# Last attention layer of a two-layer model: slots of eight heads with two blocks each, all scores of a slot together

## The reference

```
def _L1_ffn_ref(x, Wa, Wp, w_std, w_rec):           # C = 512, 16 heads of D = 32 (24 + 8)
    col_scale = concat([repeat(s_std, 24), repeat(s_std, 24), ones(C), repeat(s_rec, 8), repeat(s_rec, 8)])
    fused = x @ (Wa * col_scale)                    # Q_std, K_std, V, Q_low, K_low
    q_tail = where(w_rec > 0.1, K_low, Q_low)       # k_tail the other way round
    Qf, Kf = concat([Q_std, q_tail]), concat([K_std, k_tail])
    scores = Qf @ Kf.T * scale, masked causally (112 x 112 for each head)
    y = softmax(scores) @ V, heads side by side
    return y @ Wp
x = x + tanh(g_ffn[1]) * _L1_ffn_ref(_layernorm(x), Wa, Wp, w_std, w_rec)
```

## Time and profile before

| | us |
|---|---|
| runs | 2291.36, 2295.45, 2295.76 (median 2295.45) |
| the profiled execution | 2293.49, its span 2291.7 |
| busy, share of the span: PEld, DVE, ACT, POOL | 76%, 56%, 51%, 29% |
| mean granted PE clock | 0.966 |

### The profile page before, as it was taken

One profiled execution on the slowest core, in us unless ns is written; L12 is line 12 of the kernel. 1 busy time (PEld: TensorE's weight loads), 2 busy tenths in 40 slices (PEclk: granted clock), 3 DMA queues, 4 the chain that ended last, 5 costly groups with the idle time before them and its releaser, 6 DMA issues. The chain is left out here.

```text
span 2291.7 us, 38460 instructions
## 1 busy us (share of the span) xinstructions
PE 2136.5 (93%) x13464; PEld 1734.4 (76%) x13464; DVE 1273.0 (56%) x2475; ACT 1170.7 (51%) x3025; POOL 664.6 (29%) x814
## 2 busy tenths in 40 slices
PE   6999999999989999999969995999999997888997
PEld 4777777777767888898858875888888886666775
DVE  4555555555544554564345555777777774555454
ACT  4666666666553333353324435666776663433343
POOL 1423524425321000000014443555555551111121
PEclk9999999999999999999979997999999998899897
DMA  4433435525237210100033433332222312101010
GB/s 144 133 103 121 146 88 164 157 84 165 79 120 264 91 65 1 65 1 28 1 115 110 125 118 114 102 102 94 93 70 99 102 51 85 54 25 41 17 31 27
DMA packets 167397, 205.96 MB, mean 90 GB/s; under 512 B 63680, under 2 KB 105664, under 8 KB 166752
## 3 DMA queue, kind: packets, MB, share of 16 engines
q1 hardware_dynamic: 167264, 204.15, 28.0%
HBM read 128.13 MB, written 75.99 MB: 89 GB/s over the span
## 5 line engine op out<-in xcount | busy, mean ns | idle before, releaser
L1696 POOL TENSOR_TENSOR c_probs<-c_probs,c_rsum 112x375 f32<-112x375 f32 x256 | 212.8, 834 | 232.1 <-DVE c_rsum L1806 226.2
L1802 DVE TENSOR_REDUCE c_nmax<-c_score 112x1 f32<-112x375 f32 x256 | 136.2, 533 | 98.5 <-PE c_score L1872 98.5
L536 ACT ACTIVATE a_probs<-a_score,a_nmax 112x375 f32<-112x375 f32 x256 | 144.0, 571 | 59.6 <-DVE a_nmax L690 59.6
L1750 ACT ACTIVATE c_pT_hi<-c_turned 125x336 fp32r<-125x336 f32 x256 | 115.4, 451 | 109.1 <-PE c_turned L1880 109.0
L1191 ACT ACTIVATE b_silu<-b_gate,b_ug_scale 128x512 f32<-128x512 f32 (+1 forms) x64 | 40.6, 635 | 250.7 <-PE b_up L1297 250.6
L2100 ACT ACTIVATE f_probs<-f_score,f_nmax 112x112 f32<-112x112 f32 x256 | 87.1, 352 | 151.1 <-DVE f_nmax L2181 151.1
L543 ACT ACTIVATE a_pT<-a_turned 125x672 f32<-125x672 f32 x128 | 93.6, 731 | 135.3 <-PE a_turned L878 135.3
L1248 DVE SCALAR_TENSOR_TENSOR b_hidden<-b_up,b_ug_scale,b_silu 128x512 f32<-128x512 f32 (+1 forms) x64 | 43.7, 683 | 205.3 <-ACT b_silu L1191 205.3
L1743 ACT ACTIVATE c_probs<-c_score,c_nmax 112x375 f32<-112x375 f32 x256 | 148.0, 578 | 0.0
L2068 POOL TENSOR_TENSOR f_probs<-f_probs,f_rsum 112x448 f32<-112x448 f32 x64 | 60.0, 938 | 296.9 <-DVE f_rsum L2186 296.9
L847 PE MATMUL a_shared<-a_w_lo,a_kT_hi 128*125 128x512 f32 x384 | 135.5, 434 | 0.0
(11 more groups left out here) (299 smaller groups left out, 5947.4 us busy)
## 6 DMA issues: line engine op xcount, KB each, us to landing
q<-q_qT SPq DMA_DIRECT2D x14, 1024.0 KB
c_q_raw<-q SPq DMA_DIRECT2D x16, 896.0 KB
k<-ab_stage SPq DMA_DIRECT2D x16, 752.0 KB, 4.1
c_k_raw<-k SPq DMA_DIRECT2D x16, 752.0 KB
v<-ab_stage SPq DMA_DIRECT2D x48, 250.0 KB
c_v_raw<-v SPq DMA_DIRECT2D x16, 750.0 KB
ab_lead<-in_ctx_dram SPq DMA_DIRECT2D x16, 672.0 KB
wug<-a_ug_turned SPq DMA_DIRECT2D x32, 256.0 KB, 3.5
```

The lines of the kernel that those rows point to most:

```text
L536: last = act.activation(probs[:, n % 2, i, :], score[0:S, i, 0:T], ACT.Exp, bias=nmax[:, b % 2, h:h + 1], accum_out=sums[:, b % 2, h:h + 1])
L1696: pool.tensor_tensor(probs[:, h % AHEAD, :], probs[:, h % AHEAD, :], rsum[:, p, h:h + 1].broadcast_to([S, T]), ALU.mult).then_inc(scaled, 1)
L1750: act.activation(pT[0][:, g % 2, :, j, :], src, ACT.Copy).then_inc(pT_hi, 1)
L1802: dve.tensor_reduce(nmax[:, p, h:h + 1], score[h % AHEAD][0:S, 0:T], axis=AX.X, op=ALU.max, negate=True).then_inc(max_done, 1)
```

## The change

A slot (u) is now two quads, eight heads. PE's order in slot u is: all four halves of scores of quads 2u+2 and 2u+3 (first halves, then second halves), weigh(2u-2), weigh(2u-1), turn(2u), the first block of the slot, turn(2u+1), the other blocks, the projection, and last the activations (`x`), one a slot for the groups 2 and 3 and two a slot for group 1. From slot 2 on every slot has two blocks. The `probs` ring has four buffers and the `v` ring five. `v0` leaves the prologue, and the `v` weights come after k3 in all queues. DVE's order in slot u is: finish, low parts of the slot before's second block and x, maximum(2u+2), probs_copy(2u), maximum(2u+3), out_lo, reciprocal(2u+2), low part of the first block, probs_copy(2u+1), reciprocal(2u+3). The sizes, the instructions' shapes and their number are the same.

```diff
-    SETS, RING, V_RING = 2, 3, 6
-    SLOTS = B * G
+    SETS, RING, V_RING = 2, 4, 5
+    QUADS = B * G
+    SLOTS = QUADS // 2
+    SPAN = SLOTS // NG
...
-    weights = ("q0", "k0", "q1", "k1", "v", "q2", "k2", "q3", "k3", "p")
-    START = {-1: "x0 x1 x2 x3 q0 k0 q1 k1 v0 q2 k2 q3 k3", 0: "v1", 1: "v2", 3: "v3"}
-    FIRST_SCORES = {"q1": (0, 0), "k1": (0, 1), "v0": (1, 0), "q2": (1, 1)}
-    SECOND_TURNED = {1: "x0", 2: "x1 x2", 3: "x3"}
-    TURNED = {-10: "x0", -6: "x1", -2: "x2", 2: "x3"}
-    LATER = {4: "q0", 5: "k0", 7: "q1", 8: "k1", 9: "v0", 11: "q2", 12: "k2", 13: "q3", 15: "k3", 16: "v1", 17: "v2", 19: "v3"}
+    weights = ("q0", "k0", "q1", "k1", "q2", "k2", "q3", "k3", "v", "p")
+    FIRST_BLOCKS = "x0 x1 x2 x3 q0 k0 q1 k1 q2 k2 q3 k3"
+    SCORES_AFTER = "q2"
+    START = {0: "v0 v1", 1: "v2 v3"}
+    SECOND_TURNED = {0: "x0 x1", 1: "x2 x3"}
+    TURNED = {-2: "x0", -1: "x1", 0: "x2", 1: "x3"}
+    LATER = {2: "q0", 3: "k0 q1", 4: "k1", 5: "q2 k2", 6: "q3", 7: "k3 v0", 8: "v1", 9: "v2 v3"}
+    def blocks(u):
+        found = [(0, name) for name in START.get(u, "").split()]
         for g in range(1, NG):
+            found += [(g, name) for name in LATER.get(u - SPAN * (g - 1), "").split()]
         return found
+    def turns(u):
+        return [(g, name) for g in range(1, NG) for name in (SECOND_TURNED if g == 1 else TURNED).get(u - SPAN * (g - 1), "").split()]
+    def finished(u):
+        return [b for b in range(B) if u == 2 * b + 2]
...
@@ scalar: the slots
+            for u in range(SLOTS + 2):
+                for g, name in blocks(u - 1)[1:] + turns(u - 1):
+                    item_hi(g, name)
+                for b in finished(u):
+                    out_hi(b)
+                if u + 1 < SLOTS:
+                    exps(2 * u + 2)
+                    exps(2 * u + 3)
+                for g, name in blocks(u)[:1]:
+                    item_hi(g, name)
+                if u == 0:
+                    weights_hi("p")
@@ vector: from weights_lo("k2") on, and the slots
+            item_lo(0, "q2")
+            weights_lo("q3")
             maximum(0)
+            item_lo(0, "k2")
             weights_lo("k3")
             maximum(1)
+            reciprocal(0)
+            item_lo(0, "q3")
+            weights_lo("v")
+            reciprocal(1)
+            item_lo(0, "k3")
+            for n in range(BPG):
+                normalize(BPG + n)
+            for u in range(SLOTS + 2):
+                for b in finished(u - 1):
+                    finish(b)
+                for g, name in blocks(u - 1)[1:] + turns(u - 1):
                     item_lo(g, name)
+                if u + 1 < SLOTS:
+                    maximum(2 * u + 2)
+                if u < SLOTS:
+                    probs_copy(2 * u)
+                if u + 1 < SLOTS:
+                    maximum(2 * u + 3)
+                for b in finished(u):
+                    out_lo(b)
+                if u + 1 < SLOTS:
+                    reciprocal(2 * u + 2)
+                for g, name in blocks(u)[:1]:
+                    item_lo(g, name)
+                if u < SLOTS:
+                    probs_copy(2 * u + 1)
+                if u + 1 < SLOTS:
+                    reciprocal(2 * u + 3)
+                if u == 0:
                     weights_lo("p")
+                if u % SPAN == 4 and u // SPAN + 2 < NG:
                     for n in range(BPG):
+                        normalize(BPG * (u // SPAN + 2) + n)
@@ tensor
+            def next_scores(u):
+                for half in range(2):
+                    for t in (2 * u, 2 * u + 1):
+                        scores(t, half)
+            for g, name in first_blocks:
                 run_item(g, name)
+                if name == SCORES_AFTER:
+                    next_scores(0)
+            for u in range(SLOTS + 2):
+                if u + 1 < SLOTS:
+                    next_scores(u + 1)
+                if 0 < u <= SLOTS:
+                    weigh(2 * u - 2)
+                    weigh(2 * u - 1)
+                if u < SLOTS:
+                    turn(2 * u)
+                for g, name in blocks(u)[:1]:
                     run_item(g, name)
+                if u < SLOTS:
+                    turn(2 * u + 1)
+                for g, name in blocks(u)[1:]:
+                    run_item(g, name)
+                for b in finished(u):
                     project(b)
+                for g, name in turns(u):
+                    run_item(g, name)
```

More of the change, by code:

```diff
@@ L1936, in phase_d @@
     scale = float(HD) ** -0.5
[L1937 to L1946 removed]
+    weights = ("q0", "k0", "q1", "k1", "q2", "k2", "q3", "k3", "v", "p")
[7 more added lines that the diff above has]
+        found = [(0, name) for name in START.get(u, "").split()]
         for g in range(1, NG):
[L1948 to L1960 removed]
+            found += [(g, name) for name in LATER.get(u - SPAN * (g - 1), "").split()]
+        return found
+    def turns(u):
+        return [(g, name) for g in range(1, NG) for name in (SECOND_TURNED if g == 1 else TURNED).get(u - SPAN * (g - 1), "").split()]
+    def finished(u):
+        return [b for b in range(B) if u == 2 * b + 2]
+    first_blocks = [(0, name) for name in FIRST_BLOCKS.split()]
+    order = first_blocks + [item for u in range(SLOTS) for item in blocks(u) + turns(u)]
+    uses = first_blocks + [use for u in range(SLOTS + 2) for use in blocks(u) + [(b, "y") for b in finished(u)] + turns(u)]
+    FIRST = len(first_blocks)
     def number(g, name):
@@ L2064, in _ @@
         def _(pool):
-            for t in range(SLOTS):
+            for t in range(QUADS):
                 r = t % RING
@@ L2118, in _ @@
             item_hi(0, "q1")
-            weights_hi("v")
+            weights_hi("q2")
             item_hi(0, "k1")
-            weights_hi("q2")
+            weights_hi("k2")
+            item_hi(0, "q2")
+            weights_hi("q3")
             exps(0)
[L2123 to L2126, removed]
+            item_hi(0, "k2")
             weights_hi("k3")
             exps(1)
[L2129 to L2135, removed]
-                    item_hi(g, name)
-                if t + 2 < SLOTS:
-                    exps(t + 2)
-                if t == 1:
+            item_hi(0, "q3")
+            weights_hi("v")
+            item_hi(0, "k3")
+            for u in range(SLOTS + 2):
+                for g, name in blocks(u - 1)[1:] + turns(u - 1):
+                    item_hi(g, name)
+                for b in finished(u):
[6 more added lines that the diff above has]
+                if u == 0:
                     weights_hi("p")
@@ L2216, in _ @@
             item_lo(0, "q1")
-            weights_lo("v")
+            weights_lo("q2")
             item_lo(0, "k1")
+            weights_lo("k2")
+            item_lo(0, "q2")
+            weights_lo("q3")
             maximum(0)
[L2220 to L2224, removed]
+            item_lo(0, "k2")
             weights_lo("k3")
             maximum(1)
-            for name in ("k2", "q3", "k3"):
-                item_lo(0, name)
@@ L2229, in _ @@
[L2229 to L2242, removed]
-                    item_lo(g, name)
[L2244 to L2247, removed]
+            reciprocal(0)
@@ L2326, in weigh @@
                 if t == 0:
-                    pe.wait_ge(work_lo, split_number(0, "q3"))
+                    pe.wait_ge(work_lo, split_number(0, "k3"))
                 if i == 0:
```

18 lines of the change are left out of this document (1 added, 17 removed).

## The result

| | before | changed |
|---|---|---|
| median of the runs, us | 2293.96 (2291.36 to 2295.76, 4 runs) | 2233.68 (2232.39 to 2238.74, 4 runs) |
| the profiled execution, its span | 2293.49, 2291.7 | 2232.39, 2230.7 |
| mean granted PE clock | 0.966 | 0.974 |

The forecast was 2260, 33 us less than before.

What follows compares the result with a forecast made beforehand. PE was taken as the bound, losing time to stalls and low clock around `x` turnings. Slot 2 at 1991.8, plus 214.4, minus 3.6, plus 51.6 gave 2254.2 against 2287.5, -33 us: 2260 us, 8 in 10 within 2249 to 2277.

Steps and rivals of the forecast that it cites:

- Part 1: Middle, slots 2 to 25: the new block order removes all 12 PE gaps and the low clock; 214.4 us.
- rival a: Middle: gaps of 22.3 us go, some 12 us of slowness stay as turnings lower the clock; 2272; chance .10.
- Part 2: Middle scores: joins between equal halves save .15 us a double slot, -3.6 us in all (bounds 0 and -10).
- Part 3: Before slot 2: PE idles 4.9 us for k3, twice 1 to 3 more, mostly low clock; slot 2 at 1991.8.
- the table's second row: Phase start to slot 2: forecast 71.9 us, measured 67.3, difference -4.6.
- Part 4: From the last `v3` to the last projection's end: score loop decides, 51.6 us as before, bounds 46 and 56.
- (b): Score joins in the middle save all of .14 us each; 2254; chance .13.
- (c): Prologue costs more: DVE's hold on `xn` some 8 us longer or clock not back until slot 3; 2269; chance .13.
- (d): Middle: banks not cleared, one gap per `x` stays, 8 x 1.9 us, with half the low clock; 2281; chance .05.
- (e): Middle: the score loop becomes the bound and eats all gain at 10.15 us a slot; 2297; chance .05.
- The base: The forecast was made from the profiled execution, 2293.49 us, 2.0 below the median of 2295.45.

## Why the prediction was wrong

**Part 1, the order of the blocks: right, size nearly.** No bank waits from slot 2 to 25, the clock is 1.00. The terms of the sum (gaps and low clock together, 22.3 and about 12 us, as rival a had them) are 34; the run with only the order changed is 40 us faster. The rest is within what the kernel before varies by itself, 8 us between two executions. One count in the prediction is off: from 1986 to 2167 its trace has thirteen gaps on PE, of 24.3 us. The twelve of 22.3 leave out one of 2.01 at 1988.80, behind the last `x` of group 1, which stays in the run with only the order changed.

**Part 2, all scores together: the step that failed.** It took .15 us a double slot, 3.6 in all, with bounds of 0 and 10. Measured is .80, 16.0 us in 20 of the 24 double slots (against the run with only the order changed), and 20.1 in all 24 (214.4 - 194.3). Two errors. The first is the choice within its own bounds: the three joins between scores gave .43, the upper bound itself, since a run of scores pays about .14 beyond its halves and there is one run where there were four. I had held against it, two halves .56 apart; quad by quad that distance does come (.57), and the row said how dear that order is, not that the interleaved one saves little. The second is that only joins between scores were counted. Moving all scores together also puts weighs beside weighs (.66 to .53) and a turn ahead of a block instead of scores (.48 to .32 or .36). The earlier trace rows held only the old prices (.33 and .48), each with what follows it there, and I carried them into the new order as if they were the instructions' own. How the turns' part divides between turn and block is open (the run with a turn moved). The Trainium skill (TensorE: Matmul & The Clock Gate, The mechanism) says that a weight load overlaps running matmuls only where the row group differs. The prediction took from it that the joins save nothing, but only two of the three are on the same rows; the one in the middle, from first halves to second halves, is on different ones. The runs agree with the rule as to which pair overlaps more: two halves on different rows take .45 us together, two on the same rows .73. But those on the same rows save .13 against two apart (.86), where the rule taken alone would give nothing.

**Part 3, the prologue: the waits right, the clock too low.** 4.9 forecast and 4.73 measured for k3's low half; the copy 51.2 us after the phase's start by the estimate (1971.1 - 1919.9), turn(1) at 51.3 (1965.23 - 1913.92). Of the 1 to 3 us twice more it was one wait of 5.29. But PE was taken to run mostly at 1.2 GHz until 1985, 65 us into the phase; it was back at 2.4 some 4 us after turn(1), 55 us into it. Slot 1 took 9.6 us (1971.63 to 1981.20) where the prediction had 13.3: that is 3.7 of the 4.6 us of the table's second row. The runs with `xn` loaded first confirm the cause of the second wait: it goes, and 6 us of the phase with it.

**Part 4, the tail: right.** 51.6, taken over from the kernel before, against 51.0. The projection waits for `out_lo` (1.07, .67, .67 and 1.32 us), and the clock is 0.73:

```profile
2180.26 1.59 PE L2362 MATMUL f_work<-f_wp_hi,f_oT_hi 128*112 128x512 f32 x4 [1.07 <-DVE f_oT_lo L2203]
...
2196.22 2.05 PE L2362 MATMUL f_work<-f_wp_hi,f_oT_hi 128*112 128x512 f32 x4 [0.67 <-DVE f_oT_lo L2203]
```

From projection to projection it is 16.0 and 17.0 us, where 16 to 16.5 were worked out for the low clock. Blocks moved into this tail make it 5.6 us shorter in one profile and 4.5 in the other, so it is bound by the score loop and not by PE's work.

**The rivals.** (a) the low clock in the middle: no, 1.00 with 48 turns and eight `x`. The Trainium skill (TensorE: Matmul & The Clock Gate, Part 4: PE-mode transpose) says that a transpose does not count as PE-busy the same way. That finds no support in this stretch, where transposes stand between matmuls; nothing here tests transposes alone. (b) the joins at their full size: its direction came, at twice its price, since it too counted only the score joins. (c), (d) and (e) did not come: slot 2 started 67.3 us into the phase, PE waits for no bank from there on, and for no `f_probs` in the middle.

**The base.** 6.0 us of the miss are that the profiled execution of before had entered the phase later than any other. Its total was ordinary all the same (2293.49, median 2293.96): the other profiled execution entered 5.0 us earlier and lost 8.1 in the phase. That these two nearly made up for each other in the base is chance. Even without it the time would have been below 2249: 2233.7 + 6.0 = 2239.7. The range failed by Part 2.

## What to carry to other kernels

Where small matmuls of different tile shapes alternate on a bound PE, price a reordering by the distance of starts at every change of kind in the slot, not only at those between the instructions that are moved together: here a run of scores cost about .14 us beyond its halves, and two weighs side by side took .13 less than apart. Look first at which bank each use needs and when the use before the last is read by another engine; two calls in another order gave two thirds of the gain. And take the time lost to the clock after gaps as uncertain by itself (6.8 us between two profiles of twelve equal gaps), in the forecast as well as in the base it is made from.

## What the runs showed that I had not expected

- Two score halves on different 64 rows that meet take .45 us together; two on the same rows .73 (.34 and .39); a lone one .43. An order of second half and next first half, with cover for `first_pair`, might be shorter still than the 1.29 of the changed kernel. It was not tried.
- A second half that waits for its first half's semaphore (`first_pair`) starts .56 to .57 us after the start of the first (the earlier trace rows and the quad by quad kernel). In the changed kernel the third half of each slot starts .57 after the first too (1981.20 to 1981.77), so the same wait may still hold it back, with the other first half in between.
- Two executions with the same twelve gaps differ by 8.1 us in the phase and 6.8 in the middle. With the gaps gone the middle repeats within .2 us in seven profiles, while the front still drifts by up to 2 us.
- Half a microsecond of waits can be dear: with the second turn moved, a slot with waits of .26 and .23 us takes 2.4 us longer, at a granted clock of 0.84.
